# A delta-rule attention layer on one core: TensorE's small products taken as whole stages

## The chip, the cores and the metric

The kernel runs on one core of a Trainium2 chip. Its time is the device time in microseconds (us) of one execution. The engines are TensorE (PE; its weight loads are shown apart as PEld), VectorE (DVE), ScalarE (ACT), GpSimd (POOL) and SyncE (SP), which issues the DMAs.

## The reference, cut to what matters

```python
x = L0_attn_x                                   # 4 x 4096 x 512, float32
x = x + layernorm(attn(layernorm(x), Wv, Wo, Wg, Wb))
x = x + layernorm(ffn(layernorm(x), weight, ln_gamma, ln_beta))

# attn: 16 heads of 32; rk is x's head vectors, normalised; wk is rk one row later
v, gate, beta = x @ Wv.T, sigmoid(x @ Wg.T), sigmoid(x @ Wb.T)
def step(S, inp):                               # over the 4096 rows
    pred = einsum('bhk,bhkd->bhd', wk_t, S)
    err = (v_t - pred) * b_t[..., None]
    S = S + wk_t[..., None] * err[..., None, :]
    return S, einsum('bhk,bhkd->bhd', rk_t, S) * g_t[..., None]
# out @ Wo.T

# ffn: the weight is rounded to -1, 0, 1; xn * 128 / max|xn| is clipped, multiplied, scaled back
```

## The kernel before, in words

`setup` turns the weights and splits them into two float16 parts. `attention` handles the 4096 rows in 128 tiles of 32 rows of each of the 4 batches, 128 partitions in all. `feed_forward` then reads the result back from DRAM, in 32 groups. The change is in `attention` alone.

The recurrence is done a tile at a time, in matrix form. For tile n TensorE multiplies the state by the tile's keys (`predict`, 16 products, line 949), the result is copied to `rhs` by ScalarE (line 611) and turned back by TensorE (`turn_back`, line 956), VectorE subtracts it from the value (line 831, semaphore `rhs_done`), and TensorE multiplies by the inverse of a 32x32 system for each head and batch (`solve_error`, 64 products, line 962). ScalarE copies the result to `err` (line 688), TensorE adds keys times error to the state in `ps_s` (`update`, 64 products, line 1024), and ScalarE copies that to `state` (line 709) for the next tile. In float32 each product shows as two matmuls and two weight loads. So a half of `solve_error` or `update` is 64 matmuls in the trace, and the whole is 128.

The inverses come from VectorE, which eliminates column after column (lines 800 and 808) for pairs of tiles, so that its work repeats every two steps: an even step transposes `m_t` (line 752), an odd one ends with the transpose to `t_t` (line 816).

A step of the loop is written out for all engines, in program order on each engine, with everything unrolled. Step j works on tile j in the recurrence, and on later and earlier tiles in the rest: `LAG_V = 7` (value product, keys, gates of tile j + 7), `LAG_GRAM = 6` (product of the keys with each other), `LAG_TURN = 9` (transposes of x), `LAG_PART = -1`, `LAG_OUT = -2` (transposes of the output), `LAG_Y = -3` (output product). All three groups are live from step 3 to step 120. `value(first, end)` and `output(first, end)` issue some of the 12 wide products (128x512, float16) of `ps_v` and `ps_y` (both line 925); they are put between the other stages. `SHARE` is 3.

The path of the keys is: TensorE transposes `key` into `ps_v` (line 1011, semaphore `kt_psum`), ScalarE copies it to `kt` (line 702, `kt_done`), SP issues four DMAs `kbd<-kt` (line 456) that lay the blocks out in `kbd`, and in the next step TensorE takes the gram product (line 981), after `gram_ready` has waited for them. ScalarE then copies `gram` (line 674), GpSimd masks it to `m_t` (line 571) for VectorE. SP's queue holds in each step, in this order: `x_in`, two small `gate` moves, four DMAs of `key_bd` (line 448, for the next `predict`), four of `kbd`, `x_res`, the store of `x1`.

TensorE's order in a step before is: predict; 4 value products; turn_back; 2 value; gram; 3 value; first half of the error; 3 value; second half of the error; transposes of x (line 1003); key transposes; 3 output; first half of the update; 3 output; second half; transposes of the output (line 1048); gate products; 6 output.

Of the kernel before, what the change touches and what calls it, by code (L numbers as in the profile page):

```python
# [20 lines left out]
ALU = mybir.AluOpType  # L21
# [8 lines left out]
P = 128  # L30
# [242 lines left out]
def attention(nc, io, k):  # L273
    with ExitStack() as ctx:
# [197 lines left out]
        def _(pool):  # L472
# [5 lines left out]
            def step(base, j):  # L478
# [73 lines left out]

                n, l, live = on(base, j, LAG_NORM)
# [18 lines left out]

                n, l, live = on(base, j, LAG_PART)
                if live:
                    wait(pool, s["ohi_done"], n + 1)
                    wait(pool, s["ot_psum"], n - 1)
                    pool.tensor_tensor(o_part[:, l % 2, 1, :], o_g[:, :], o_part[:, l % 2, 0, :],  # L577
                                       ALU.subtract).then_inc(s["olo_done"], 1)
# [16 lines left out]
        def _(act):  # L595
            def step(base, j):
# [17 lines left out]
                if live:  # L614
# [5 lines left out]
                                         accum_out=y_var[:, l % 2:l % 2 + 1]).then_inc(s["y_var"], 1)  # L620
                n, l, live = on(base, j, LAG_STATS2)
# [31 lines left out]

                n, l, live = on(base, j, LAG_PART)
                if live:
                    wait(act, s["o_done"], n + 1)
                    wait(act, s["ot_psum"], n - 1)
                    nc.scalar.activation(o_part[:, l % 2, 0, :], o_g[:, :], ACT.Copy).then_inc(s["ohi_done"], 1)

# [10 lines left out]
                n, l, live = on(base, j, LAG_GRAM)  # L670
                if live:
                    wait(act, s["gram_psum"], n + 1)
                    wait(act, s["mt_done"], n)
                    nc.scalar.activation(gram[:, :, :].rearrange("p i h -> p (i h)"), ps_gram[:, :], ACT.Copy).then_inc(s["gram_done"], 1)  # L674

                n, l, live = on(base, j, LAG_V)
                if live:
                    wait(act, s["v_psum"], n + 1)
                    wait(act, s["o_done"], n - 7)
                    wait(act, s["rhs_done"], n - 7)  # L680
                    nc.scalar.activation(val[:, l, :], ps_v[:, :], ACT.Copy).then_inc(s["v_done"], 1)

                n, l, live = on(base, j, 0)
                if live:
                    wait(act, s["err_psum"], n + 1)
                    wait(act, s["s_psum"], n - 1)
                    wait(act, s["pred_done"], n - 1)
                    nc.scalar.activation(err[:, l % 2, :], ps_chain[:, :], ACT.Copy).then_inc(s["err_done"], 1)  # L688

# [7 lines left out]

                n, l, live = on(base, j, LAG_V)
# [6 lines left out]
                n, l, live = on(base, j, 0)  # L705
                if live:
                    wait(act, s["s_psum"], n + 1)
                    wait(act, s["pred_psum"], n)
                    nc.scalar.activation(state[:, (l + 1) % 2, :], ps_s[:, :], ACT.Copy).then_inc(s["state_done"], 1)  # L709
# [29 lines left out]
        def _(dve):  # L739
# [81 lines left out]
            def step(base, j):  # L821
# [3 lines left out]
                multipliers(base, j)  # L825
                n, l, live = on(base, j, 0)
# [7 lines left out]
                m, k_l, k_live = on(base, j, LAG_TURN)  # L834
                if k_live:
                    wait(dve, s["sq_done"], m + 1)
                    wait(dve, s["ss_done"], m)
                    dve.tensor_reduce(ss_raw[:, :], heads(x_sq[:, k_l % 2, :]), AX_X, ALU.add).then_inc(s["ss_sum"], 1)
# [45 lines left out]
        def _(pe):  # L884
# [48 lines left out]
            def step(base, j):  # L933
# [34 lines left out]
                if v_live:  # L968
                    wait(pe, s["gexp_done"], v)
                    wait(pe, s["xt_done"], upto(v + 2))  # L970
# [17 lines left out]
                if v_live:  # L988
                    last.then_inc(s["v_psum"], 1)
# [368 lines left out]
```

## Time and profile before

| what | us |
|---|---|
| runs (3) | 2324.87, 2329.17, 2331.81 |
| median | 2329.17 |
| span of the profiled execution | 2313.7 |
| PE busy | 2084.1 (90%) |
| DVE busy | 1992.1 (86%) |
| ACT busy | 1774.0 (77%) |
| POOL busy | 1729.0 (75%) |

The profiled execution has no time of its own beside its span: the median of the runs lies 15.5 us above the span. The span counts from the first to the last instruction. The recurrence runs from about 139 us to about 1950 us, the feed-forward part after it.

### The profile page before, as it was taken

What the parts mean: (1) busy time and instruction counts of PE and PEld (TensorE: products, weight loads), DVE (VectorE), ACT (ScalarE), POOL (GpSimd) and SP (SyncE); (2) the same over time, 40 slices, a digit from 0 to 9 for tenths busy, and PEclk for the clock granted to TensorE, in tenths of its full rate; (3) what the DMA queues carried; (4) which work ended last, traced back from release to release, by engine and by line L of the source; (5) the groups of instructions that cost most, each with busy time, mean ns of one, the idle gap of its engine ahead of it and who ended that gap; (6) DMA issues with size and microseconds to landing.
All of it is one profiled execution on the core that took longest, in us unless ns stands there. A gap on an engine that the chain in (4) does not pass through costs nothing. (4 is left out here: it accounts for less than half of the span.)

```text
span 2313.7 us, 123730 instructions
## 1 busy us (share of the span) xinstructions
PE 2084.1 (90%) x50216; PEld 1316.0 (57%) x50216; DVE 1992.1 (86%) x5810; ACT 1774.0 (77%) x3756; POOL 1729.0 (75%) x3099
## 2 busy tenths in 40 slices
PE   1679999999999999999999999999999987499997
PEld 1346666666666666666655656566666654255554
DVE  5388999999999999999889999899999994588886
ACT  3667888888888888888877878788888744477775
POOL 2668888888888888888888888888888854244443
PEclk7789999999999999999999999999999988799999
DMA  2122333333333333333333333333333222488885
GB/s 86 48 65 80 98 100 98 98 98 95 99 97 99 94 94 95 95 94 94 93 91 93 94 96 91 94 97 96 100 96 99 82 78 67 150 225 229 225 231 129
DMA packets 156632, 247.69 MB, mean 107 GB/s; under 512 B 39544, under 2 KB 39552, under 8 KB 156064
## 3 DMA queue, kind: packets, MB, share of 16 engines
q1 hardware_dynamic: 156064, 239.78, 36.6%
q8 instruction: 397, 6.50, 1.2%
q14 instruction: 171, 1.40, 0.2%
HBM read 104.40 MB, written 67.11 MB: 74 GB/s over the span
## 5 line engine op out<-in xcount | busy, mean ns | idle before, releaser
L800 DVE TENSOR_TENSOR ps_elim<-ps_elim,sys 128x30 f32<-128x30 f32 (+14 forms) x1920 | 543.3, 326 | 0.7
L808 DVE TENSOR_TENSOR sys<-sys,ps_elim 128x30 f32<-128x30 f32 (+14 forms) x1920 | 534.6, 316 | 1.0
L925 PE MATMUL ps_v<-wv,xt 128*128 128x512 f16 x1536 | 435.2, 389 | 39.6 <-DVE rhs L831 16.5
L925 PE MATMUL ps_y<-wo,ot 128*128 128x512 f16 x1536 | 406.1, 386 | 17.3 <-DVE x L852 9.5
L962 PEld LDWEIGHTS ps_chain<-rhs,t_t 32*32 32x32 f32 x16384 | 257.3, 144 | 110.6 <-issue 110.5
L962 PE MATMUL ps_chain<-rhs,t_t 32*32 32x32 f32 x16384 | 286.1, 218 | 13.9 <-issue 8.5
L709 ACT ACTIVATE state<-ps_s 128x512 f32<-128x512 f32 x128 | 76.5, 598 | 265.6 <-PE ps_s L1024 263.6
L1024 PEld LDWEIGHTS ps_s<-err,key_b 32*32 32x32 f32 x16384 | 172.1, 106 | 147.4 <-issue 147.2
L1310 PE MATMUL ps_f<-wq,f_xq 128*128 128x512 f16 x1024 | 242.5, 381 | 6.8 <-DVE f_xq L1276 6.8
L538 POOL TENSOR_TENSOR x_part<-x_hat,x_part 128x512 f16<-128x512 f32 x128 | 148.7, 1162 | 131.6 <-ACT x_hat L645 111.5
L1024 PE MATMUL ps_s<-err,key_b 32*32 32x32 f32 x16384 | 205.5, 195 | 34.2 <-issue 34.2
L925 PEld LDWEIGHTS ps_v<-wv,xt 128*128 128x128 f16 x1536 | 121.0, 99 | 188.4 <-issue 120.5
L925 PEld LDWEIGHTS ps_y<-wo,ot 128*128 128x128 f16 x1536 | 130.2, 98 | 130.3 <-issue 26.3
L831 DVE TENSOR_TENSOR rhs<-val,ps_chain 128x512 f32<-128x512 f32 x128 | 87.4, 682 | 121.1 <-PE ps_chain L956 121.1
L1158 POOL TENSOR_TENSOR f_y_veps<-f_y_var,y_eps 128x1 f32<-128x1 f32 x128 | 53.6, 418 | 184.3 <-ACT f_unread L1191 183.4
L585 POOL TENSOR_TENSOR pred<-val,err 128x512 f32<-128x512 f32 x128 | 163.1, 1274 | 11.3 <-ACT err L688 11.2
L571 POOL TENSOR_TENSOR m_t<-gram,b_mask 128x512 f32<-128x512 f32 x128 | 163.5, 1277 | 5.3 <-ACT gram L674 5.2
L512 POOL TENSOR_TENSOR b_mask<-gates,neg_mask 128x512 f32<-128x512 f32 x128 | 135.5, 1059 | 32.0 <-DVE gates L879 31.9
L1310 PEld LDWEIGHTS ps_f<-wq,f_xq 128*128 128x128 f16 x1024 | 100.2, 98 | 102.0 <-DVE f_xq L1276 7.5
L577 POOL TENSOR_TENSOR o_part<-o_g,o_part 128x512 f16<-128x512 f32 x128 | 148.5, 1160 | 0.0
L949 PE MATMUL ps_chain<-key_bd,state 128*32 128x128 f32 x4096 | 139.9, 277 | 4.3 <-issue 2.8
L714 ACT ACTIVATE ot<-ps_gram 128x1024 f16<-128x1024 f16 x128 | 130.9, 1022 | 16.8 <-PE ps_gram L1048 16.7
(163 smaller groups left out, 5123.6 us busy)
## 6 DMA issues: line engine op xcount, KB each, us to landing
x_in<-in_L_attn_x SPq DMA_DIRECT2D x128, 256.0 KB
kbd<-kt SPq DMA_DIRECT2D x512, 64.0 KB, 2.1
key_bd<-key_t SPq DMA_DIRECT2D x512, 64.0 KB, 2.4
x_res<-in_L_attn_x SPq DMA_DIRECT2D x128, 256.0 KB
x_scratch<-x SPq DMA_DIRECT2D x128, 256.0 KB, 6.3
f_x<-x_scratch SPq DMA_DIRECT2D x32, 1024.0 KB, 7.6
out<-f_res SPq DMA_DIRECT2D x128, 256.0 KB, 3.9
gate<-gates SPq DMA_DIRECT2D x128, 7.9 KB
```

The lines of the kernel that those rows point to most:

```text
L512: pool.tensor_tensor(b_mask[:, :, :], beta.unsqueeze(1).to_broadcast([P, C, H]), k["neg_mask"][:, :].unsqueeze(2).to_broadcast([P, C, H]), ...
L538: pool.tensor_tensor(x_part[:, l % 2, 1, :], x_hat[:, l % 4, :], x_part[:, l % 2, 0, :], ALU.subtract).then_inc(s["xlo_done"], 1)
L571: pool.tensor_tensor(m_t[:, :, l % 2, :], gram[:, :, :], b_mask[:, :, :], ALU.mult).then_inc(s["mt_done"], 1)
L577: pool.tensor_tensor(o_part[:, l % 2, 1, :], o_g[:, :], o_part[:, l % 2, 0, :], ALU.subtract).then_inc(s["olo_done"], 1)
L585: pool.tensor_tensor(pred[:, :], val[:, l, :], err[:, l % 2, :], ALU.subtract).then_inc(s["pred_done"], 1)
L800: dve.tensor_tensor(tmp, factors(r, c, first, end)[:, c - first:C - 1 - first, c - first:c - first + 1].to_broadcast(shape), sys[:, r, c:c ...
L808: dve.tensor_tensor(dst, dst, tmp, ALU.add).then_inc(elim_done[r], 1)
L925: last = pe.matmul(out, lhs[:, a, kb, :], weights[:, w, kb, :], start=(i == 0), stop=(i == 3 * KB - 1))
L949: last = pe.matmul(out, state[:, l % 2, HD * h:HD * h + HD], key_bd[:, :, h, :], start=True, stop=True)
L962: last = pe.matmul(ps_chain[q, e], t_t[q, l // 2 % 2, :, l % 2, h], rhs[q, e], start=True, stop=True)
L1024: last = pe.matmul(ps_s[q, e], key_b[q, l, e], err[q, l % 2, e], start=(isinstance(n, int) and n == 0 and h == 0), stop=True, skip_group_c ...
L1310: last = pe.matmul(ps_f[i][:, :], xq[:, r % 2, a, kb, P * i:P * i + P], k["wq"][:, kb, :], start=(m == 0), stop=(m == 2 * KB - 1))
```

## The change

TensorE takes its step in another order: predict; gram; turn_back; 7 value products; the whole error; 5 value; transposes of x; the whole update; key transposes; 6 output; transposes of the output; gates; 6 output. `gram_ready` is asked directly behind predict, `error_ready` before the seventh value product as before the ninth earlier. ScalarE takes `gram` behind `y_var`, `err` behind `x_sq`, then `o_part`, `val`, the small norm operations, `xt`, `state`, `kt`. GpSimd takes the low part of `o_part` ahead of the norm operations. VectorE takes the sum of squares (`ss_raw`) ahead of `rhs`. No operation is added or removed.

```diff
+                    pool.tensor_tensor(o_part[:, l % 2, 1, :], o_g[:, :], o_part[:, l % 2, 0, :],
+                                       ALU.subtract).then_inc(s["olo_done"], 1)
...
+                    nc.scalar.activation(gram[:, :, :].rearrange("p i h -> p (i h)"), ps_gram[:, :], ACT.Copy).then_inc(s["gram_done"], 1)
...
+                    nc.scalar.activation(err[:, l % 2, :], ps_chain[:, :], ACT.Copy).then_inc(s["err_done"], 1)
...
+                    nc.scalar.activation(state[:, (l + 1) % 2, :], ps_s[:, :], ACT.Copy).then_inc(s["state_done"], 1)
...
+                    dve.tensor_reduce(ss_raw[:, :], heads(x_sq[:, k_l % 2, :]), AX_X, ALU.add).then_inc(s["ss_sum"], 1)
...
                 predict()
-                if v_live:
-                    wait(pe, s["gexp_done"], v)
-                    wait(pe, s["xt_done"], upto(v + 2))
-                value(0, SHARE + 1)
-                turn_back()
-                value(SHARE + 1, SHARE + 2)
                 gram_ready(base, j)
-                value(SHARE + 2, SHARE + 3)
                 if m_live:
...
                     last.then_inc(s["gram_psum"], 1)
-                value(SHARE + 3, 3 * SHARE - 1)
+                turn_back()
+                if v_live:
+                    wait(pe, s["gexp_done"], v)
+                    wait(pe, s["xt_done"], upto(v + 2))
+                value(0, 2 * SHARE)
                 error_ready(base, j)
-                value(3 * SHARE - 1, 3 * SHARE)
+                value(2 * SHARE, 2 * SHARE + 1)
                 solve_error(0)
-                last = value(3 * SHARE, 4 * SHARE)
+                last = solve_error(1)
+                if live:
+                    last.then_inc(s["err_psum"], 1)
+                last = value(2 * SHARE + 1, WHOLE)
...
+                update_ready(base, j)
+                update(0)
+                last = update(1)
+                if live:
+                    last.then_inc(s["s_psum"], 1)
+
                 if v_live:
                     wait(pe, s["key_done"], v + 1)
...
-                output(0, SHARE - 1)
-                update_ready(base, j)
-                output(SHARE - 1, SHARE)
-                update(0)
-                output(SHARE, 2 * SHARE)
-                last = update(1)
-                if live:
-                    last.then_inc(s["s_psum"], 1)
+                output(0, 2 * SHARE)
```

## Rows read from the trace of the kernel before

**Rows 1.** The page: busy time, share, instructions; a DMA queue's packets and MB.

```profile
PE 2084.1 (90%) x50216; PEld 1316.0 (57%) x50216; DVE 1992.1 (86%) x5810; ACT 1774.0 (77%) x3756; POOL 1729.0 (75%) x3099
...
q8 instruction: 397, 6.50, 1.2%
```

**Rows 2.** All waits of the execution: us in total, times, longest.

```profile
DVE rhs L831 <- PE ps_chain L956: 121.1, 67, 8.5
```

**Rows 3.** Timeline of DVE, 590 to 619 us: start, length, then the instruction.

```profile
590.67 0.68 DVE L831 TENSOR_TENSOR rhs<-val,ps_chain 128x512 f32<-128x512 f32 x1
...
603.25 0.69 DVE L831 TENSOR_TENSOR rhs<-val,ps_chain 128x512 f32<-128x512 f32 x1 [1.25 <-PE ps_chain L956]
...
618.58 0.67 DVE L831 TENSOR_TENSOR rhs<-val,ps_chain 128x512 f32<-128x512 f32 x1
```

**Rows 4.** Timeline of PE, one step from 600.65 to 614.55 us, the main stages.

```profile
600.65 1.08 PE L949 MATMUL ps_chain<-key_bd,state 128*32 128x128 f32 x32
...
602.56 0.66 PE L956 MATMUL ps_chain<-ident,rhs 128*128 128x128 f32 x4
...
603.57 1.08 PE L981 MATMUL ps_gram<-kbd,kt 128*32 128x128 f32 x32
604.59 0.82 PE L925 MATMUL ps_v<-wv,xt 128*128 128x512 f16 x3
605.34 1.11 PE L962 MATMUL ps_chain<-rhs,t_t 32*32 32x32 f32 x64
606.38 0.82 PE L925 MATMUL ps_v<-wv,xt 128*128 128x512 f16 x3
...
608.17 0.62 PE L1003 MATMUL ps_gram<-ident_half,x_part 128*128 128x128 f16 x8
608.68 0.63 PE L1011 MATMUL ps_v<-ident,key 128*128 128x128 f32 x4
609.15 0.81 PE L925 MATMUL ps_y<-wo,ot 128*128 128x512 f16 x3
609.89 0.75 PE L1024 MATMUL ps_s<-err,key_b 32*32 32x32 f32 x64
610.57 0.82 PE L925 MATMUL ps_y<-wo,ot 128*128 128x512 f16 x3
...
612.04 0.61 PE L1048 MATMUL ps_gram<-ident_half,o_part 128*128 128x128 f16 x8
...
613.17 1.46 PE L925 MATMUL ps_y<-wo,ot 128*128 128x512 f16 x6
614.55 1.08 PE L949 MATMUL ps_chain<-key_bd,state 128*32 128x128 f32 x32
```

**Rows 5.** The page's groups: busy us, mean ns of one, idle before.

```profile
L962 PE MATMUL ps_chain<-rhs,t_t 32*32 32x32 f32 x16384 | 286.1, 218 | 13.9 <-issue 8.5
...
L1024 PE MATMUL ps_s<-err,key_b 32*32 32x32 f32 x16384 | 205.5, 195 | 34.2 <-issue 34.2
```

**Rows 6.** Timeline of ACT and SP, 600 to 614 us: the keys' copy, key DMAs.

```profile
603.17 7.04 SPq L448 DMA_DIRECT2D key_bd<-key_t  x4
...
609.92 0.62 ACT L702 ACTIVATE kt<-ps_v 128x512 f32<-128x512 f32 x1
...
610.56 2.83 SPq L456 DMA_DIRECT2D kbd<-kt  x4
```

**Rows 7.** Tile kbd, 400 to 1800 us: ns of an issue (min, median, max), and landing.

```profile
L456 SPq DMA_DIRECT2D kbd<-kt x390: 507/592/2049, 400.0 to 1799.6; - x195
...
DMA to landing us min/median/max: 1.9/2.1/3.8
```

**Rows 8.** Timeline of PE, 1000 to 1017 us: two idle times inside the update.

```profile
1001.84 0.31 PE L1024 MATMUL ps_s<-err,key_b 32*32 32x32 f32 x11 [0.62 <-issue]
...
1016.44 0.31 PE L1024 MATMUL ps_s<-err,key_b 32*32 32x32 f32 x12 [0.86 <-issue]
```

**Rows 9.** Waits of PE, 400 to 1800 us: us in total, times, longest.

```profile
PE ps_s L1024 <- issue: 28.7, 34, 1.2
```

## What the change is expected to do

> **What bounds the kernel now.** I read the page first. TensorE is busy for 90% of the span and VectorE for 86% [rows 1], so a share alone does not name the bound, and both have to be followed through a step. In the list of all waits, the one to see is VectorE's. Before `rhs` it stood 121.1 us for TensorE's turned prediction, in 67 cases [rows 2]. 67 is about half of the 128 tiles, so this happens every other step. The timeline of VectorE says why. From `rhs` at 590.67 to the next at 603.25 there are 12.58 us, the last 1.25 of them idle. From 603.25 to 618.58 there are 15.33 us with no wait before `rhs` [rows 3]. The kernel has two kinds of steps. In the long one VectorE's eliminations set the pace and TensorE waits for `rhs`. In the short one VectorE waits for TensorE. A pair takes 27.91 us, or 13.96 a step.
>
> What TensorE saves in a long step is thus worth nothing. In a short step only a stretch of it counts: from the start of the error products, behind one `rhs`, to the end of the turn_back in front of the next. VectorE's own work is 27.91 - 1.25 = 26.66 us a pair, 13.3 a step. No order of TensorE can go below that.
>
> The timeline of one step of TensorE gives the pieces [rows 4]. Differences of starts: predict and 4 value products 1.91 us, turn_back and 2 value products 1.01, gram 1.02, 3 value 0.75, half of the error 1.04, x transposes 0.51, key transposes 0.47, 3 output 0.74, half of the update 0.68, 3 output and the other half 1.47, 6 output 1.38. 6 wide products in 1.38 against 3 in 0.75 make 0.21 each and 0.12 for a group, most of it where small products follow.
>
> The third thing is what has no releaser. 28.7 us in 400 to 1800 us were idle inside the update with "issue" as the reason, 34 times [rows 9], such as 0.62 and 0.86 us, 14.60 us apart, with 11 and then 12 matmuls left behind them [rows 8]. Queue q8 shows what that is. It fetched 6.50 MB in 397 packets, and TensorE has 2 x 50216 instructions [rows 1], so a packet holds 253 of them. A step holds some 760, so three packets. The idle time therefore sits at a packet's border, which creeps by one matmul with its load a step. It appears where the packet before was used up fastest.
>
> **The change, part by part.** No operation is added or removed.
>
> *Fewer changes of stage.* The page has 218 ns for one error matmul and 195 ns for one of the update [rows 5]. A half of the error runs 1.11 us to its last end and 1.04 to the next stage [rows 4]. Its last start is at 1.11 - 0.22 = 0.89, so 63 intervals of 14.1 ns and a tail of 0.15. A whole is 127 x 0.0141 + 0.15 = 1.94 instead of 2.08. For the update 0.75 - 0.195 = 0.56 gives 8.9 ns and a tail of 0.12. A whole is 1.27 instead of 1.36 to 1.4. Behind predict the tail is 1.08 - 0.27 = 0.81 to about 1.01, or 0.20, and it goes if gram, of the same shape, follows without a pause (else it stays). I take it as gone. The value groups go from four to two and the output groups from three to two: 3 x 0.12 = 0.36. In sum 0.14 + 0.1 + 0.2 + 0.36 = 0.8 us of TensorE's 13.9 a step.
>
> *What of that lies on the path that counts.* Before, from error start to the end of turn_back: 614.55 - 605.34 = 9.21 us, then 1.91, then about 0.5 for turn_back, 11.6. It held 3 + 12 + 4 wide products. After, it holds 5 + 12 and the gram. Gram comes in with 1.02, two wide products go with 0.42, predict's tail goes with 0.20, two groups go with 0.24 net, and error and update save 0.24. That is -0.1, and I take 0.2 us off in a short step, with bounds of 0 and 0.4. So moving gram ahead of turn_back eats nearly all that the whole stages give.
>
> *The keys' DMAs.* This is the largest term. Before, between the key transposes (608.68) and the next gram lie 614.55 - 608.68 = 5.87 us, and 1.91 and 1.01 more, 8.8 in all [rows 4]. After, gram follows predict and the transposes follow the update. From the update's end there are the transposes 0.47, 6 output 1.3, the output's transposes and the gates 0.75 (the 1.13 between 612.04 and 613.17 less some 0.4 in which they stood), 6 output 1.38 and predict 0.8: 4.7 us. In that time ScalarE must copy the state (about 0.6 as well, it is now ahead) and the keys (0.62 [rows 6]), done some 1.2 us after the update. Then SP issues four DMAs. They took 2.83 us in one step [rows 6]. An issue has a median of 592 ns and a minimum of 507, and landing takes 2.1 [rows 7]. With starts of 2.83 - 0.59 = 2.24 us for the first three, the blocks are there 1.2 + 2.24 + 2.1 = 5.5 us after the update. TensorE stands 5.5 - 4.7 = 0.8 us before gram. At the least issue time it is 1.2 + 1.52 + 1.9 - 4.7 = 0. With an issue at its maximum of 2.05 us it is 2.3; I keep 1.3 as the upper bound, as the median is far from that maximum. Queued behind this wait on TensorE are turn_back, and so `rhs`, and everything else. SP itself is free by then: `key_bd` issues after predict and ended 610.21 [rows 6], 8.5 us after predict's end at 601.66, and the keys' copy now ends some 9 us after it.
>
> In a pair this gives +0.8 - 0.2 = +0.6 in the short step. In the long step TensorE has 15.33 us for 13.1 + 0.8, so nothing. That is 0.3 us a step.
>
> *Instruction packets.* 256 instructions of the error now last 1.94 us. Before, with value products between the halves, they lasted 1.04 + 0.75 + 1.04 = 2.83. For the update it is 1.27 against 0.68 + 0.76 + 0.71 = 2.15. A border always lies somewhere in such a stretch, so each of the two stages loses between 0 and 0.88 us of cover, half on average, 0.88 a step together. In long steps VectorE hides it. So 0.44 a step is the upper bound, the lower is 0 (a wait before gram gives the fetch its time), and I take 0.4, near the upper, since the update's borders already stall today.
>
> The Trainium skill, Runtime: NRT & Kernel Launch, section "Instruction fetch mechanics", says that instructions come in 16 KiB blocks of 256 and that crossing a block's border is mostly hidden. This trace agrees on the block (253 a packet) and not on the second point (28.7 us of idle in one line, rows 9). By the Trainium skill this term would be 0.
>
> *The other engines' orders.* ScalarE's `gram`, `err` and `state` go ahead, and `val` and `kt` follow them. GpSimd's `o_part` is now behind ScalarE's copy of the error, and the norm operations and the next key are queued behind it. They are needed a step later, which hides up to a microsecond or so, and I cost them at 0. If that cover is gone, VectorE waits for `key` in its long step, 0.5 us. VectorE's sum of squares moves from behind `rhs` to ahead of it. In a long stretch it leaves behind one `rhs` and enters before the next, so the sum stands. In the short one it uses part of the 1.25 us of waiting. Cost 0, at most 0.7 where that wait is gone.
>
> **Sum.** 0.3 + 0.4 = 0.7 us a step over the 118 full steps, 83 us. The profiled span of 2313.7 becomes 2397, and with the 15.5 us by which the median lies above it, 2412. The bounds of the terms give -0.2 to +1.4 a step, 2305 to 2495.
>
> **The rivals.**
>
> *Faster (0.14).* The four issues are quick, the blocks land before gram, and the borders fall in wide products. The short step is then 0.2 shorter, 0.1 a step, and half of the present stalls go. In the update these are 28.7 us [rows 9] over some 96 steps (1400 / 14.6), 0.30 a step, so 0.15. 0.25 x 118 = 30 us, 2299. It speaks for it that a least issue makes the wait 0, and TensorE does save 0.8. It decides when TensorE waits less than 0.2 us before gram. Against it stand the 592 ns median and the 2.83 us of rows 6.
>
> *Only the gram's wait (0.13).* Fetching is hidden as before, since the wait gives it time. 0.3 x 118 = 35 us, 2364. The rule of the Trainium skill, Runtime: NRT & Kernel Launch, section "Instruction fetch mechanics", would give this one.
>
> *SP's round closes (0.10).* Late `kbd` issues push `x_res` and the store back, and the four `key_bd` issues behind them take 7.04 us [rows 6], so the next predict waits as well. With 0.5 us a step on top, 1.2 x 118 = 142, 2471. Against it: the blocks of `key_bd` have several us before predict now.
>
> *VectorE hides all (0.06).* If only the 13.96 of the pair counts and TensorE's wait falls into the long step, the time is unchanged, 2329.
>
> *Forecast (0.57).* Both terms, 2412.
>
> **Numbers.** Three runs of this kernel differ by 0.3%, so less than 0.3% (7 us) can't be told from no change. Slower: 0.57 + 0.13 + 0.10 = 0.80. Same: 0.06. Faster: 0.14. The range is from 2325, which leaves out most of the faster case, to 2470, which leaves out half of SP's.
>
> **What would show it.** In the changed profile: a wait of TensorE (line of gram, or of the stage with it) on the DMA `kbd<-kt` of 50 to 100 us in total. "Issue" idle time inside the whole error and the whole update, together twice the 28.7 us or more in the middle 1400 us. `rhs` to `rhs` on VectorE still 15.3 us in long steps, and over 13 in short ones. Half of the changes of stage gone: error about 1.94, update about 1.27. I am wrong if gram starts right behind predict, or if long steps grow: then ScalarE's or GpSimd's order is what counts.

## The result, and the profile after

The kernel became slower: 2515.1 us (median of four runs, 2503.6 to 2523.4) against 2327.0 (four runs, 2323.0 to 2331.8). The ratio is 1.081, interval 1.077 to 1.085. The forecast was 2412, with a range up to 2470, so the direction was right and the size was not. The profiled execution has a span of 2501.9 us, against 2313.7 before: 188 us more instead of 83.

The page of the changed kernel (busy us, share, count; the code queue; the clock in tenths over 40 slices; three groups of matmuls):

```profile
PE 2104.6 (84%) x50216; PEld 1401.2 (56%) x50216; DVE 1977.1 (79%) x5810; ACT 1804.8 (72%) x3756; POOL 1731.2 (69%) x3099
PEclk7779999999999999998999899999999997699999
q8 instruction: 397, 6.50, 1.1%
L962 PE MATMUL ps_chain<-rhs,t_t 32*32 32x32 f32 x16384 | 265.6, 217 | 31.8 <-issue 25.6
L974 PE MATMUL ps_gram<-kbd,kt 128*32 128x128 f32 x4096 | 148.1, 288 | 132.3 <-DMA kbd<-kt 132.1
L1014 PE MATMUL ps_s<-err,key_b 32*32 32x32 f32 x16384 | 209.0, 199 | 62.8 <-issue 56.2
```

Counts and code are those of before [rows 1]. Both engines that were near the bound are now less busy. So the time is in waits, and two stand in the groups: 132 us of gram for the keys' DMA, and 82 us of "issue" in error and update. All waits of the whole span, totals and counts:

```profile
DVE rhs L836 <- PE ps_chain L956: 186.3, 76, 11.1
DVE gates L879 <- ACT g_den L724: 171.4, 82, 10.6
PE ps_gram L974 <- DMA kbd<-kt: 132.1, 109, 3.9
```

VectorE's wait for the turned prediction grew from 121.1 us [rows 2] to 186.3. The gram waits 109 times in 128 steps, so in most of them and not in every second one. VectorE's timeline over three steps shows the same:

```profile
479.97 0.69 DVE L836 TENSOR_TENSOR rhs<-val,ps_chain 128x512 f32<-128x512 f32 x1 [2.89 <-PE ps_chain L956]
495.06 0.69 DVE L836 TENSOR_TENSOR rhs<-val,ps_chain 128x512 f32<-128x512 f32 x1 [0.24 <-PE ps_chain L956]
509.83 0.69 DVE L836 TENSOR_TENSOR rhs<-val,ps_chain 128x512 f32<-128x512 f32 x1 [2.92 <-PE ps_chain L956]
524.74 0.69 DVE L836 TENSOR_TENSOR rhs<-val,ps_chain 128x512 f32<-128x512 f32 x1
```

The steps are 15.09, 14.77 and 14.91 us. Before they were 12.58 and 15.33 in turn, 13.96 on average [rows 3]. VectorE now stands nearly 3 us in one kind of step and hardly at all in the other, and both kinds last 14.8 to 15.1 us. Something else has become the pace. TensorE's timeline of one of these steps, with SP's line for the keys, names it:

```profile
493.36 1.08 PE L974 MATMUL ps_gram<-kbd,kt 128*32 128x128 f32 x32 [1.67 <-DMA kbd<-kt]
494.37 0.66 PE L956 MATMUL ps_chain<-ident,rhs 128*128 128x128 f32 x4
494.86 1.67 PE L925 MATMUL ps_v<-wv,xt 128*128 128x512 f16 x7
496.46 2.02 PE L962 MATMUL ps_chain<-rhs,t_t 32*32 32x32 f32 x128
498.42 1.25 PE L925 MATMUL ps_v<-wv,xt 128*128 128x512 f16 x5
499.51 0.61 PE L1000 MATMUL ps_gram<-ident_half,x_part 128*128 128x128 f16 x8
500.05 1.64 PE L1014 MATMUL ps_s<-err,key_b 32*32 32x32 f32 x128
501.62 0.66 PE L1028 MATMUL ps_v<-ident,key 128*128 128x128 f32 x4
502.12 1.46 PE L925 MATMUL ps_y<-wo,ot 128*128 128x512 f16 x6
...
505.55 1.08 PE L949 MATMUL ps_chain<-key_bd,state 128*32 128x128 f32 x32
508.13 1.08 PE L974 MATMUL ps_gram<-kbd,kt 128*32 128x128 f32 x32 [1.50 <-DMA kbd<-kt]
...
502.40 0.59 ACT L707 ACTIVATE kt<-ps_v 128x512 f32<-128x512 f32 x1
...
503.01 2.42 SPq L456 DMA_DIRECT2D kbd<-kt  x4
```

This is a closed round: each part waits only for the one before it, and its end sets its next start. The gram starts at 493.36; from its start the products up to the end of the key transposes take 8.9 us (to 502.28), ScalarE's copy ends at 502.99, SP issues until 505.43, and after the landing of the last DMA the next gram starts at 508.13: 14.77 us. In this step no part of the round waits for VectorE. How long the four DMAs of this round took from issue to landing:

```profile
DMA to landing us min/median/max: 1.9/2.2/3.2
```

The gram needs all four, so the longest counts, and that is the last one issued.

The second part of the loss is later. `rhs` to `rhs` from the first and last start in each stretch and their count:

| stretch, us | before | after |
|---|---|---|
| up to 400 | 18 steps of 13.92 | 15 of 15.49 |
| 400 to 1000 | 41 of 14.36 | 39 of 14.91 |
| 1000 to 1800 | 54 of 14.50 | 48 of 16.53 |

1.57 us over the steps of the first stretch are 24 us, 0.55 over some 40 steps 22, and 2.03 over 49 steps 100. `rhs` runs from 141.2 to 1949.4 before and from 157.3 to 2134.0 after, 168.5 us longer, which leaves 23 us for the last 23 steps. The first `rhs` is 16.1 us later and the rest of the program 3.6 longer: 188.2 in all. TensorE's waits in 1000 to 1800, and the windows of both stretches (the last columns are clock, DMA share, GB/s):

```profile
PE ps_s L1014 <- issue: 38.2, 32, 2.1
PE ps_chain L962 <- issue: 20.5, 17, 1.8
PE ps_gram L974 <- DMA kbd<-kt: 18.5, 34, 1.6
```

```profile
400.00:1000.00 600.00, 534.76 (x15238) 371.41 (x15240) 518.42 (x1705) 490.23 (x1044) 500.50 (x886) 1.00 0.32 92
1000.00:1800.00 800.00, 693.63 (x18414) 472.38 (x18414) 639.50 (x2060) 594.08 (x1262) 605.00 (x1066) 0.93 0.29 84
```

In 400 to 1000 gram's wait was 55.3 us and the update waited for issue once, 0.2 us. In 1000 to 1800 "issue" takes over (72.0 us over all lines of TensorE, against 8.1), and the granted clock falls to 0.93, where it was 1.00 before. Such a step, on TensorE:

```profile
1057.63 1.66 PE L1014 MATMUL ps_s<-err,key_b 32*32 32x32 f32 x128
1060.97 0.60 PE L1028 MATMUL ps_v<-ident,key 128*128 128x128 f32 x4 [1.67 <-issue]
1061.40 2.68 PE L925 MATMUL ps_y<-wo,ot 128*128 128x512 f16 x6
```

Nothing releases the wait of 1.67 us behind the update, and the six output products after it take 2.68 us, not 1.46.

### The profile page after: what moved, and what is told of

The parts are those of the page before. It is cut to its first block and busy times, and to the rows that moved or that the text cites. A ratio compares the mean times of both kernels' runs of the same rounds, so it can differ in the third digit from the quotient of the medians.

```text
span 2501.9 us, 123730 instructions
## 1 busy us (share of the span) xinstructions
PE 2104.6 (84%) x50216; PEld 1401.2 (56%) x50216; DVE 1977.1 (79%) x5810; ACT 1804.8 (72%) x3756; POOL 1731.2 (69%) x3099
## 5 line engine op out<-in xcount | busy, mean ns | idle before, releaser
L925 PE MATMUL ps_v<-wv,xt 128*128 128x512 f16 x1536 | 407.3, 401 | 29.9 <-DVE rhs L836 20.3
L962 PEld LDWEIGHTS ps_chain<-rhs,t_t 32*32 32x32 f32 x16384 | 248.9, 145 | 80.0 <-issue 79.9
L962 PE MATMUL ps_chain<-rhs,t_t 32*32 32x32 f32 x16384 | 265.6, 217 | 31.8 <-issue 25.6
L714 ACT ACTIVATE ot<-ps_gram 128x1024 f16<-128x1024 f16 x128 | 131.1, 1024 | 186.3 <-PE ps_gram L1044 186.3
L974 PE MATMUL ps_gram<-kbd,kt 128*32 128x128 f32 x4096 | 148.1, 288 | 132.3 <-DMA kbd<-kt 132.1
L925 PEld LDWEIGHTS ps_v<-wv,xt 128*128 128x128 f16 x1536 | 145.4, 102 | 191.4 <-issue 74.1
L925 PEld LDWEIGHTS ps_y<-wo,ot 128*128 128x128 f16 x1536 | 145.8, 102 | 161.8 <-issue 42.2
L836 DVE TENSOR_TENSOR rhs<-val,ps_chain 128x512 f32<-128x512 f32 x128 | 87.5, 683 | 186.6 <-PE ps_chain L956 186.3
L1014 PEld LDWEIGHTS ps_s<-err,key_b 32*32 32x32 f32 x16384 | 181.1, 109 | 91.6 <-issue 74.4
L974 PEld LDWEIGHTS ps_gram<-kbd,kt 128*32 128x32 f32 x4096 | 116.4, 115 | 158.3 <-issue 158.3
L879 DVE RECIPROCAL gates<-g_den 128x32 f32<-128x32 f32 x128 | 44.8, 350 | 172.0 <-ACT g_den L724 171.4
L625 ACT ACTIVATE gram<-ps_gram 128x512 f32<-128x512 f32 x128 | 76.3, 596 | 123.2 <-PE ps_gram L974 122.2
```

The source lines that it names most:

```text
L714: nc.scalar.activation(ot[:, l % 2, :, :, :].rearrange("p a k t -> p (a k t)"), ps_ot[:, :].bitcast(F16), ACT.Copy).then_inc(s["ot_done"], 1)
L925: last = pe.matmul(out, lhs[:, a, kb, :], weights[:, w, kb, :], start=(i == 0), stop=(i == 3 * KB - 1))
L962: last = pe.matmul(ps_chain[q, e], t_t[q, l // 2 % 2, :, l % 2, h], rhs[q, e], start=True, stop=True)
L974: last = pe.matmul(out, kt[:, m_l % 2, g, q], kbd[:, m_l % 2, :, g, q], start=True, stop=True)
L1014: last = pe.matmul(ps_s[q, e], key_b[q, l, e], err[q, l % 2, e], start=(isinstance(n, int) and n == 0 and h == 0), stop=True, skip_group_c ...
```

## The experiments

A packet is a block of 256 TensorE instructions as they are fetched, and its border is where one block ends and the next has to be there. Two causes were to be told apart: the keys' round in front of the gram, and the borders of instruction packets in the whole stages. The orders of the other engines were the third suspect. Each time is a median, each ratio is to the kernel before on the same chip.

**Four edits of the changed kernel.** The first takes the key transposes ahead of the update, and ScalarE's `kt` ahead of `state`.

```diff
+                if v_live:
+                    wait(pe, s["key_done"], v + 1)
...
+                    last.then_inc(s["kt_psum"], 1)
                 update_ready(base, j)
                 update(0)
```

> The changed kernel with the key transposes back ahead of the update on TensorE, and ScalarE's copy of the keys ahead of its copy of the state; nothing else. Theory A (the round from gram over the update, the key transposes, ScalarE, SP's four issues and the landing back to gram paces every step): the keys' copy ends about 2 us earlier in the round, TensorE's wait before gram falls from 132 us to under 20, steps in the undisturbed stretch of 400 to 1000 us go from 14.8 to about 14.0, the time to 2440 or less. Theory B (packets of instructions and the clock that falls behind them do most of it): steps of 1000 to 1800 us stay at 16.6 and the time is not under 2480.

2514.7 us (the median of three executions; a fourth took 2533.8), ratio 1.078 (1.071 to 1.085): no gain in sum, where theory A had 2440 or less. Gram's wait fell from 55.3 to 18.0 us in 400 to 1000, and from 18.5 to 3.0 in 1000 to 1800. But there the update's wait for issue rose from 38.2 to 66.9:

```profile
PE ps_s L1014 <- issue: 66.9, 34, 2.4
```

By stretches the edit did three things. Up to 400 us the steps fell from 15.49 to 14.51 us. In 400 to 1000 they stayed (14.87 against 14.91), although gram waited 37 us less: TensorE waited 11.6 us more for issue (19.7 against 8.1), and 13.7 us for `val` and 7.3 for `rhs`, which it had not before. In 1000 to 1800 they rose from 16.53 to 17.12.

The second keeps the order but puts 3 products between the halves of the error and of the update again.

```diff
                 solve_error(0)
+                value(2 * SHARE + 1, 3 * SHARE + 1)
                 last = solve_error(1)
...
                 update(0)
+                output(0, SHARE)
                 last = update(1)
```

> The changed kernel with 3 value products between the two halves of the error again and 3 output products between the two halves of the update; key transposes and gram stay where the change put them. Theory B (whole stages use a packet of instructions up faster than the next arrives): idle time with the reason issue falls from 71 us in 1000 to 1800 us to under 35, the steps there from 16.6 to about 15.4, the clock there back to 1.00, the time to 2450 to 2475. Theory A: the round over the keys is no shorter, the wait before gram stays, and the time stays over 2490.

2562.0 us, 1.100 (1.097 to 1.102): worse. Theory B had wanted idle time for issue under 35 us in 1000 to 1800 and the clock back at 1.00. It was 75.4 us in all (60.4 in the update), as in the changed kernel (72.0), at a clock of 0.98, and gram's wait there was 47.9. Undoing the whole stages alone doesn't bring the time back, and here it didn't shorten the idle time for issue either. Steps of 400 to 1000 went from 14.91 to 15.62 us; why the kernel is 47 us slower than the changed one was not taken apart.

The third takes 4 value products and turn_back ahead of the gram, near their old place.

```diff
                 predict()
+                value(0, SHARE + 1)
+                turn_back()
                 gram_ready(base, j)
```

> The changed kernel with gram behind 4 value products and turn_back again, 2 value products behind it; key transposes stay behind the update. Theory A: gram has some 1.4 us more cover and leaves the path from turn_back to turn_back, so its wait falls under 40 us and steps in 400 to 1000 us are about 14.0; time about 2430. If the place of gram itself costs nothing, the time stays at 2515.

2500.8 us, 1.073 (1.067 to 1.078). Theory A had about 2430. In 1000 to 1800 no wait of the gram for its DMA is listed any more, and the update's wait for issue is 67.4 us. The stretches are as with the first edit: 14.53 us a step up to 400, 14.92 in 400 to 1000, 17.02 after.

The fourth has TensorE's order of the changed kernel and the orders of before on ScalarE, GpSimd and VectorE.

> TensorE in the changed order, ScalarE, GpSimd and VectorE in the order of before. If the matching orders are what costs (ScalarE's copy of the state ahead of that of the keys, the normalisation later), the time falls under 2480. By theory A only the copy of the keys comes 0.5 us earlier, 2450 to 2500. If the matching orders help, as they are named, the time rises over 2530.

2613.2 us, 1.120 (1.114 to 1.126): 98 us slower than the changed kernel. The new line among TensorE's waits in 1000 to 1800 was the update for ScalarE's copy of the error, 29.3 us in 43 steps.

**Borders made to stand still.** None of these four could be read in sum, as long as the borders crept through the step. A step has 770 TensorE instructions (380 matmuls, 380 weight loads, and 10 for semaphore waits that need an instruction of their own), two more than three packets of 256. Two of the semaphore waits repeat what an earlier wait of the step has established. Without them the step has 768, and the borders stay where they are.

```diff
                     wait(pe, s["gexp_done"], v)
-                    wait(pe, s["xt_done"], upto(v + 2))
+                    if not on(base, j - 1, LAG_OUT)[2]:
+                        wait(pe, s["xt_done"], upto(v + 2))
...
-                    wait(pe, s["gram_done"], upto(j + LAG_GRAM + 1))
+                    if not on(base, j, LAG_TURN)[2]:
+                        wait(pe, s["gram_done"], upto(j + LAG_GRAM + 1))
```

Counted from predict, the borders then stand at instructions 40, 296 and 552: in predict, in the error and in the update. On the changed kernel:

> The changed kernel without two waits a step of TensorE that other waits of TensorE already imply. A step then has 768 instructions instead of 770, three packets, and the borders of the packets stand still in the step, about where they were in steps 5 to 10 (inside predict, inside the error, inside the update, each with slow stages before them). Theory F (the time lost in 1000 to 1800 us comes from borders that have crept to the ends of the two whole stages, and from the clock that falls behind them): all steps take about 14.8 us as those of 400 to 1000 us do, and the time is 2420, 1.04 of before. If instead something else in the later part of the recurrence is slow, its steps stay at 16 to 17 us and the time over 2490.

2487.4 us, 1.069 (1.066 to 1.073), 28 us less, where 2420 was expected: the idle time for issue fell from 72.0 to 6.9 us in 1000 to 1800, and the steps there to 15.59 us, but in 400 to 1000 they rose from 14.91 to 15.43. On the kernel before:

> The kernel before without the same two waits a step, borders standing still. Theory F: the idle times with the reason issue go, steps of 13.4 to 14.0 us throughout, time 2285 to 2300, 0.98 of before. If packets cost before nothing: 2327.

2318.5 us, 0.995 (0.993 to 0.997), where 2285 to 2300 was expected. No idle time for issue is left in 400 to 1800, yet only some 10 us were gained: TensorE now stands 43.8 us there for the keys' DMAs, where it stood 2.1 us before. Then the first again, with 68 unused transposes ahead of everything on TensorE, which move the borders to 161, 417 and 673: to the start of the error, in front of the last value product behind it, and 5 products (10 matmuls) in front of the update's end.

```diff
+            for _ in range(68):
+                pe.transpose(banks[1][:, 0:P], k["ident"][:, :], k["ident"][:, :])
```

> As the changed kernel without the two waits, and with 68 transposes more (136 instructions) at the very start of TensorE's program, while it waits for the weights. They cost nothing themselves and move the standing borders by 136, to about the end of gram, the end of the error and the end of the update. Theory F: every step is like those of 1050 to 1500 us, 16 to 17.5 us, the clock is below 1.00 in all of the recurrence, and the time is 2620 to 2720. If packets are not the cause: the same time as without the 68 transposes.

2668.5 us, 1.145 (1.143 to 1.148). The place of the borders alone is worth 181 us. Steps are 16.9 us in both stretches ((987.9 - 411.6) / 34 and (1785.2 - 1006.1) / 46). Its timeline, and the windows of the same step:

```profile
1214.75 0.39 PE L927 MATMUL ps_v<-wv,xt 128*128 128x512 f16 x1 [0.28 <-issue]
1214.98 0.61 PE L1003 MATMUL ps_gram<-ident_half,x_part 128*128 128x128 f16 x8
1215.52 1.40 PE L1017 MATMUL ps_s<-err,key_b 32*32 32x32 f32 x118
1218.69 0.42 PE L1017 MATMUL ps_s<-err,key_b 32*32 32x32 f32 x10 [1.77 <-issue]
1219.04 1.11 PE L1031 MATMUL ps_v<-ident,key 128*128 128x128 f32 x4
1219.95 2.51 PE L927 MATMUL ps_y<-wo,ot 128*128 128x512 f16 x6
```

```profile
1205.00:1217.00 12.00, 10.83 (x344) 7.19 (x340) 11.08 (x32) 10.76 (x24) 8.51 (x18) 1.00 0.34 97
1217.00:1222.30 5.30, 3.60 (x21) 1.99 (x22) 4.23 (x15) 1.43 (x3) 4.98 (x10) 0.68 0.19 46
1222.30:1226.00 3.70, 3.70 (x86) 2.80 (x88) 1.27 (x4) 3.03 (x7) 1.92 (x3) 1.00 0.42 111
```

Between two borders lie here only the last products of values, the transposes of x and 118 matmuls of the update. They were used up by 1216.9, and the next packet's first matmul ran at 1218.69, 3.9 us after the border before it. In the windows the clock falls to 0.68 around the stall, so for most of the 5.3 us it is at 1.2 GHz, and comes back to 2.4 GHz. The key transposes then take 1.11 us instead of 0.66 and the output products 2.51 instead of 1.46: 1.5 us on top of the 1.77.

A control moves the borders by exactly one packet, with 128 transposes (256 instructions):

> Control for the run with bad borders: the changed kernel with standing borders and 128 transposes at the start, 256 instructions, so that the borders stand at 40, 296 and 552 as without any. If only the borders' place counts, 2487, within 15 us. If the additional transposes or what they do to the clock or the fetching cost, 2550 or more.

2479.5 us, 1.069 (1.065 to 1.073), like the kernel with none. It is the place and not the added work.

**The keys' round, with borders standing.** TensorE's line for the gram in 1000 to 1800 of the changed kernel with standing borders, and three rows of its timeline:

```profile
PE ps_gram L974 <- DMA kbd<-kt: 89.0, 52, 2.6
```

```profile
615.35 1.65 PE L974 MATMUL ps_gram<-kbd,kt 128*32 128x128 f32 x32 [2.13 <-DMA kbd<-kt]
616.93 1.12 PE L956 MATMUL ps_chain<-ident,rhs 128*128 128x128 f32 x4
617.84 2.31 PE L925 MATMUL ps_v<-wv,xt 128*128 128x512 f16 x7
```

The wait is there in every one of its 52 steps, 1.7 us on average. In the step shown gram, turn_back and values behind it run at the lower clock too (1.65, 1.12, 2.31 against 1.08, 0.66, 1.67). That is so in 11 of the 24 steps of 400 to 1800 us in which the wait is over 2 us, and in 4 of the others. The first and third edits were made again here, and then both.

> The changed kernel without the two waits, borders standing still, and with the key transposes and their copy ahead of the update and the copy of the state. With the packets out of the way it shows what the round over the keys costs by itself: theory A says steps of 14.8 fall to 14.0 or less and the time lies 80 to 100 us under that of the changed kernel with standing borders. If the round does not pace the steps, the two are within 20 us.

2420.5 us, 1.039 (1.036 to 1.042): 67 us less than with borders standing alone, a little under the 80 to 100 expected. Steps went from 15.43 to 15.09 us in 400 to 1000 and from 15.59 to 14.91 in 1000 to 1800.

> The changed kernel with standing borders (inside predict, the error and the update) and gram behind 4 value products and turn_back again. Theory A, the round over the keys: the wait of TensorE on the keys' DMAs, 89 us in 1000 to 1800 us with gram directly behind predict, falls under 20, and the time from 2487 to about 2400. If gram's place does not matter, 2487.

2383.7 us, 1.027 (1.023 to 1.032): 104 us less, with steps of 14.63 and 14.72. The path from the error to turn_back stays about as long by it: gram's 1.0 us leave it, and four value products of about as much come in. Its line of the same view:

```profile
PE ps_gram L980 <- DMA kbd<-kt: 27.2, 43, 1.4
```

> Standing borders, gram behind turn_back, key transposes and their copy ahead of the update and the copy of the state: of the change only the whole stages and the other engines' orders are left. Theory A: no wait on the keys' DMAs is left, about 2350 to 2370, within 2% of before. If the whole stages or the other engines' orders cost something by themselves, it stays at 2400 or more.

2401.9 us, 1.034 (1.030 to 1.039), where 2350 to 2370 was expected. Gram's wait is 6.6 us, but the key transposes, now early, wait for ScalarE's `val`, whose copy must leave `ps_v` first. One wait replaced the other, in 1000 to 1800:

```profile
PE ps_v L1024 <- ACT val L678: 58.1, 53, 1.5
```

**Whole stages alone, at two places of the borders.** The kernel before with standing borders, and only the halves put together, the 3 products behind them:

```diff
                 solve_error(0)
-                last = value(3 * SHARE, 4 * SHARE)
...
                 last = solve_error(1)
...
+                last = value(3 * SHARE, 4 * SHARE)
...
                 update(0)
-                output(SHARE, 2 * SHARE)
                 last = update(1)
...
+                output(SHARE, 2 * SHARE)
```

> The kernel before with standing borders, and of the change only the whole stages: both halves of the error behind the ninth value product and the last 3 value products behind them, both halves of the update behind the third output product and 3 output products behind them; all else as before, so ScalarE still copies the value ahead of the error. Fewer changes of stage save 0.4 us of TensorE a step: 2290 to 2320 if that shows. If the whole stages cost more than they save (the copy of the error later, packets used up faster), 2340 to 2400.

> The kernel before with standing borders and 68 transposes more at the start: borders at 161, 417 and 673 of a step, the same as in the changed kernel with bad borders. With halves of stages and wide products between them this should cost little: steps of 14.7, 2360 to 2390 (before had 14.9 us in steps 70 to 79, with these borders).

> The same with whole stages of error and update, borders at 161, 417 and 673. Theory F, whole stages use a packet up before the next has come: 0.8 us or more a step above the run with halves, 2450 to 2520, idle time with the reason issue inside the update over 60 us in 1000 to 1800 us. If whole stages alone do not make the borders dear, within 20 us of the run with halves.

| us (ratio to before) | borders at 40, 296, 552 | at 161, 417, 673 |
|---|---|---|
| in halves | 2318.5 (0.993 to 0.997) | 2362.0 (1.015 to 1.019) |
| whole | 2318.3 (0.997 to 1.002) | 2554.2 (1.098 to 1.104) |

The second column has the 68 transposes in front. At the one place whole stages bring nothing: the times are equal, and by the ratios, which allow for the two chips that they ran on, they cost 0.4% or some 10 us, about the noise. At the other they cost 192 us more than halves, more than the 2520 that was expected at most. TensorE's line for issue at the second place, in halves and then whole, 1000 to 1800:

```profile
PE ps_s L1027 <- issue: 45.1, 55, 1.2
```

```profile
PE ps_s L1027 <- issue: 81.0, 49, 2.0
```

A stall of 0.8 us a step on average in halves, with the clock at 1.00, became one of 1.65, with the clock at 0.97 (0.95 in 400 to 1000). 0.8 us cost less than their length (44 us over 118 steps is 0.37 a step). The longer ones cost all of it (236 us is 2.0 a step; the value products' 12.3 us for issue make the stall 1.9).

**The other engines' orders, with borders standing.** TensorE's order of before with the others' of the change:

> Standing borders, TensorE in the order of before, ScalarE, GpSimd and VectorE in the order of the change. If the other engines' orders cost by themselves, it is slower than 2318, 2360 or more, because they match another order of TensorE: ScalarE stands before gram, which TensorE makes later. If they are neutral, 2310 to 2330.

2651.1 us, 1.142 (1.140 to 1.145), 333 us slower than with their own orders. TensorE's and ScalarE's waits in 1000 to 1800:

```profile
PE ps_v L1012 <- ACT val L678: 77.8, 47, 1.7
```

```profile
ACT gram L625 <- PE ps_gram L982: 101.1, 46, 2.9
```

ScalarE takes `gram` first and stands there, as TensorE makes it later in that order. `err` and `val` are queued behind it, and TensorE's key transposes wait for `val`. The opposite, the better TensorE order (gram behind 4 values and turn_back) with the others' of before:

> Standing borders, TensorE in the changed order with gram late, and ScalarE, GpSimd and VectorE in the order of before. Against 2384 with the changed orders of these engines: lower (2340 or less) if their changed orders are what is left of the cost, higher (2430 or more) if ScalarE's copies of error and state need to be ahead for whole stages, the same if the rest lies in TensorE's own order.

2368.6 us, 1.020 (1.018 to 1.022), 15 us less than with the orders of the change. 10 of them are at the start, where the first `rhs` comes at 140.4 us and not at 150.3; the steps are nearly the same (14.65 and 14.63 against 14.63 and 14.72). What TensorE waits for in 1000 to 1800 is now this, in nearly every step:

```profile
PE ps_s L1016 <- ACT err L688: 42.3, 54, 0.8
```

**Two places that beat both kernels.** The order of before at two more places of the borders, by 111 and 103 unused transposes (borders at 74, 330, 586 and at 90, 346, 602).

> The kernel before with standing borders and 111 transposes more at the very start, which put the borders at instruction 74, 330 and 586 of a step (before turn_back, inside the error's first half, among the output products between the halves of the update), where steps 108 to 118 of the kernel before had them, with 13.9 us on average against 14.3. Theory F: 2270 to 2300, under both kernels. If the borders' place does not matter: 2318.

2297.4 us, 0.989 (0.985 to 0.993).

> The kernel before with standing borders at 90, 346 and 602 (103 transposes at the start): at the start of gram, in the error's second half, early in the second half of the update. The kernel before had these in steps 100 to 105, 14.1 us. About 2297 as with 74, between 2285 and 2320.

2304.8 us, 0.993 (0.990 to 0.996). The order was not touched, and the kernel is about 1% faster than before.

## Why the prediction was right in its direction and wrong in its size

**Fewer changes of stage.** Half right. The error whole takes 1.96 us to the next stage, forecast 1.94. The update takes 1.57 (500.05 to 501.62) where 1.27 was forecast by adding up the half of [rows 4]: a whole update is no faster than two halves (0.68 and 0.71). Why a product inside it is slower than in a half (199 ns busy for one against 195, and longer between starts) stays open. Predict's tail was not saved: gram stood behind it for its DMA in 38 of the 40 steps between 400 and 1000. The part of it that could be measured alone, whole stages with the order of before, where 0.4 us a step of TensorE were expected to be saved, was worth nothing (2318.3 against 2318.5).

**The path from error to turn_back.** The forecast measured a short step by it. In the changed kernel the short step is no longer set by it but by the round described next, and the two kinds of steps became alike.

**The keys' DMAs.** The wait itself was put at 0.8 us with an upper bound of 1.3, and measured 1.5 in 400 to 1000 (55.3 us in 38 steps), 132 us in total against 50 to 100. The term that was too small is the landing. "landing takes 2.1" is the median over all four DMAs of a step, but the gram waits for the last of them, and in 400 to 1000 of the changed kernel that one took 3.1 us from issue to landing (median of 40 steps). The blocks are there 6.4 us after the update and not 5.5, and TensorE has 5.1 us of other work and not 4.7.

The step that failed is what was made of the wait: "In a pair this gives +0.8 - 0.2 = +0.6 in the short step. In the long step TensorE has 15.33 us for 13.1 + 0.8, so nothing." It took the wait for a fixed lateness, added to a short step of 12.58 and free in a long one. But the gram heads a round whose next key copy lies behind the gram itself, so a late gram makes the next keys late. The sum of that round, 14.77 us, holds in each step. Measured were 14.8 to 15.1 us in both kinds: the short ones over 2 us longer, and the long ones shorter than the 15.3 that the forecast expected still to see. Against the 13.96 of [rows 3] the round costs 0.8 us a step and not 0.3.

That the round is a cause is shown by shortening it at both ends with the borders standing: 67 us back by the earlier keys, 104 by the later gram, together only 85 (the wait for `val`). In the changed kernel with its creeping borders the picture is mixed. Up to 400 us, where the steps lost 1.57 us each, gram waited 51.9 us in 22 steps, and either edit took about 1.0 us a step back (14.51 and 14.53). In 400 to 1000, where they lost 0.55, neither did (14.87 and 14.92 against 14.91): other waits took the place of gram's. So that the 0.55 is the round's is not shown.

**Instruction packets.** That whole stages use up a packet before the next is there was right (2554 against 2362 us at the same borders), and the size was not; in the second edit, though, halves with products between them did not shorten the idle time, and that stays open. "I take 0.4" spread the loss evenly, with 0.44 as its upper bound. In the trace of the changed kernel it is near 0 in 400 to 1000 (8.1 us in all, less than the 21.5 before) and, beside the keys' part, 16.53 - 14.91 = 1.6 us a step in 1000 to 1800. That is 48 x 1.6 = 78 us, against 0.4 x 118 = 47 forecast. Two things lie outside the bound. A cover that is lost "half on average" is the wrong reading, since a border moves only two instructions a step: it stays for dozens of steps where it does harm. And the stall draws the clock down, which the forecast doesn't have at all. In the windows above, this costs 1.5 us beside a stall of 1.77. The creeping adds some 28 us to the changed kernel (2515 to 2487) and 9 to the one before. But the place that it was compared with is not a best one for the changed order: with borders at 40, 296 and 552 it has steps of 15.43 us in 400 to 1000 (586.3 / 38), longer than the 14.91 with creeping borders, so the packets' whole share is not measured by that difference.

The Trainium skill, Runtime: NRT & Kernel Launch, section "Instruction fetch mechanics", says that code comes in blocks of 256 instructions and that crossing a block's border is mostly hidden. The runs agree on the block: steps of 768 hold the borders still, and 256 more instructions change nothing. They don't agree on the second point, with 181 us between two places of the same code. The Trainium skill, TensorE: Matmul & The Clock Gate, Part 1, says that an idle array falls back to 1.2 GHz; here a clock of 0.68 around a stall of 1.77 us agrees.

**The other engines' orders.** "I cost them at 0" was wrong as a statement about them alone: TensorE's new order with the old orders is 98 us slower than with the new ones, so there the new orders help, and TensorE's old order with the new ones is 333 us slower than with the old. With the gram late they cost 15 us, 10 of them at the start. What they cost or give thus hangs on TensorE's order, and no one number stands for it.

**The rivals.** None of them was it. "SP's round closes" (2471, given 0.10) came nearest: a round did close. But `key_bd` and predict were not what waited in it, the gram was, and SP's queue was only one station, 2.42 us of 14.77. "Only the gram's wait" (2364) left out the packets. Faster and unchanged are excluded.

**What is left.** By the runs with standing borders the way back is: 2487 changed, 2384 with the gram behind turn_back, 2369 with the others' old orders, 2318 with TensorE's old order (ratios to before 1.069, 1.027, 1.020, 0.995). The last 50 us (the places of the key transposes and of the wide products among the stages) were not tried one by one. The trace names a likely part: with 5 value products and the x transposes alone between the whole error and the update, the update stands 0.8 us for ScalarE's copy of the error in 54 steps of 1000 to 1800. No such wait is listed for whole stages in the order of before, which have the key transposes and 3 output products there as well. The 16 us by which the first `rhs` is later come out of the same runs: with standing borders it is at 140.4 us before, 140.4 with TensorE's new order and the gram late, 150.3 with the others' new orders as well, and 155.4 with the gram early too. So some 10 us are the other engines' orders and some 5 the gram.

## What to carry to other kernels

When a consumer of a DMA is moved earlier in a loop and its producer later, add up the whole round from consumer to consumer, the transfer and every engine between, and compare it with the step: if the producer stands behind the consumer on one engine that works in program order, the wait comes in every step and not only where the step is short. If several DMAs must land, go by the last one and not by the median of all. Count the instructions of an engine's step against the packets of 256: with a border inside a dense stage of small products, wide ones between its halves can be worth much (192 us here), a step of a whole number of packets keeps the borders still, and then their place is a setting worth trying, before any reordering is judged. Orders of engines are a set: change and time them together, and never conclude from one edit while another cause can take its gain.

## What the runs showed that was not expected

- The place of packet borders alone moved one program between 2487 and 2668 us, and with the order of before between 2297 and 2362.
- Idle times of TensorE of 1.7 to 2.0 us a step on average went with a granted clock of 0.95 to 0.98 over a stretch (three runs with standing borders), whether the wait was for issue or for the keys' DMAs. The matmuls behind one such stall took about 1.7 times as long (1.11 against 0.66 us, 2.51 against 1.46). Stalls of 0.8 us on average left it at 1.00, and so did the waits of 1.5 us in 400 to 1000 of the changed kernel.
- 128 matmuls of the update in one piece took 1.57 us in one timeline, while two halves took 0.68 and 0.71. The error showed no such thing (1.96 against twice 1.04).
